# A graph and transformer layer on one core: the message sum moved ahead of the attribute and node products, and the gathers' wait moved from the message to its sum

## The reference

```
h     = (layernorm(x) @ W.T)                       # per node, 8 heads x 32
alpha = h[src].a_src + h[dst].a_dst + sum(relu(attr @ edge_W.T + edge_b) * h[dst])   # per edge and head
alpha = leaky(alpha, 0.2);  ex = exp(alpha - max over the edges of dst)
out   = segment_sum(h[src] * ex / sum of ex over dst, dst)
```

## Time and profile before

| | |
|---|---|
| time before, median of 3 | 4190.25 us (4185.47 to 4199.82) |
| span of the profiled execution | 5158.3 us |
| PE busy | 3767.6 us (73%) |
| DVE busy | 2599.5 us (50%) |
| ACT busy | 2112.2 us (41%) |
| POOL busy | 2005.2 us (39%) |
| mean granted TensorE clock | 0.850 |

### The profile page before, as it was taken

How to read it: one execution, slowest core, us unless ns; L and a number is a source line. 1 busy time by engine, 2 the same in 40 slices (tenths; PEclk the granted TensorE clock), 3 DMA queues, 4 the chain that set the end, 5 groups by cost and what they waited for, 6 DMA issues and landing times.

```text
span 5158.3 us, 88906 instructions
## 1 busy us (share of the span) xinstructions
PE 3767.6 (73%) x22054; PEld 2527.9 (49%) x22055; DVE 2599.5 (50%) x6056; ACT 2112.2 (41%) x5703; POOL 2005.2 (39%) x2172
## 2 busy tenths in 40 slices
PE   4788997677677667677767667777766667891999
PEld 3357886344444444444434444444444444771888
DVE  5556554455555555555555555555555555440111
ACT  3212332344444444444444444444444445442332
POOL 3120000555455544455544555555554442005111
PEclk8889998788888888888888888888888888895999
DMA  4610111333333333333333333443333332102110
GB/s 151 225 44 17 34 33 49 92 99 100 97 97 101 99 99 99 97 100 100 102 100 94 101 100 99 105 102 98 102 102 100 100 101 93 72 22 59 36 36 28
DMA packets 352302, 449.27 MB, mean 87 GB/s; under 512 B 170970, under 2 KB 275163, under 8 KB 350456
## 3 DMA queue, kind: packets, MB, share of 16 engines
q0 software_dynamic: 95568, 267.78, 19.8%
q10 hardware_dynamic: 108050, 122.83, 7.8%
q1 hardware_dynamic: 148231, 53.53, 4.3%
HBM read 389.57 MB, written 55.13 MB: 86 GB/s over the span
## 4 chain that ended last, share of the span: by engine, by line
PE 39%; another core or an unknown queue 17%; issue 15%; DVE 12%; ACT 6%; ACTq 6%; DMA 3%; DVEq 1%; POOL 1%; SPq 0%; POOLq 0%
PE bank L1099 6%; PE bank L1040 5%; PE bank L1183 4%; PE bank L1195 4%; PE bank L1143 3%; PE bank L1005 3%; PE bank L1014 3%; ACT dist L770 3%; DVE prod L1460 3%; PE bank L1061 2%; ACTq L355 2%; DVE msg L1540 2%; ACTq L737 2%; PE bank L1030 2%
## 5 line engine op out<-in xcount | busy, mean ns | idle before, releaser
L514 POOL DMA_INDIRECT al<-h_tab,idx x976 | 975.4, 999 | 1021.5 <-issue 970.8
L752 ACT ACTIVATE enc<-bank,eb 128x512 f32<-128x512 f32 x880 | 555.3, 682 | 1601.5 <-remote 1338.1
L514 POOL DMA_INDIRECT gbuf<-h_tab,idx x784 | 786.5, 1003 | 821.3 <-issue 738.5
L1061 PE MATMUL bank<-prod,hsel 128*32 128x128 f32 x7040 | 336.9, 317 | 928.5 <-issue 779.0
L1040 PE MATMUL bank<-oneh_t,hbt 125*128 125x512 bf16 x2640 | 839.4, 464 | 38.0 <-issue 33.9
L1061 PEld LDWEIGHTS bank<-prod,hsel 128*32 128x32 f32 x7040 | 199.4, 122 | 1098.5 <-issue 916.4
L1460 DVE SCALAR_TENSOR_TENSOR prod<-enc,adst,bank 128x512 f32<-128x512 f32 x880 | 629.1, 736 | 25.8 <-remote 10.9
L1099 PE MATMUL bank<-msg,oneh 128*125 128x264 f32 x2352 | 613.1, 406 | 14.9 <-DVE r L1549 9.1
L1549 DVE TENSOR_TENSOR r<-r,bank 125x264 f32 x440 | 188.5, 428 | 757.8 <-remote 534.3
L1099 PEld LDWEIGHTS bank<-msg,oneh 128*125 128x125 f32 x2352 | 476.8, 204 | 154.4 <-issue 45.9
L770 ACT ACTIVATE dist<-iota_n,dtile 128x125 f32<-128x125 f32 x1760 | 551.1, 384 | 2.0 <-issue 0.5
(11 more groups left out here) (255 smaller groups left out, 5399.6 us busy)
## 6 DMA issues: line engine op xcount, KB each, us to landing
dstb<-dst ACTq DMA_DIRECT2D x440, 125.0 KB
al<-pen_d SPq DMA_DIRECT2D x1760, 4.0 KB
att<-attrx ACTq DMA_DIRECT2D x880, 24.0 KB
al<-h_tab,idx POOLq DMA_INDIRECT x976
link<-links SPq DMA_DIRECT2D x880, 0.2 KB
gbuf<-h_tab,idx POOLq DMA_INDIRECT x784
attrx<-al ACTq DMA_DIRECT2D x8, 1176.0 KB, 12.3
hsplit<-hb POOLq DMA_DIRECT2D x25, 375.0 KB, 5.2
```

Source lines behind the costliest of these rows:

```text
L514: pool.indirect_dma_start(slot(n)[:, c, :], None, h_tab, bass.IndirectOffsetOnAxis(ap=idx[g % 2][:, k:k + 1], axis=0)).then_inc(gathered[n ...
L752: m = act.activation(enc[n % 2][:, k, :], bank[k][:, :], ACT.Relu, bias=eb[:, k:k + 1])
L1061: m = pe.matmul(bank[7][32 * c:32 * c + 32, 0:128], hsel[:, i, :], prod[n % 2][:, k, c * 128:(c + 1) * 128], start=(i == 0 and k == 0), st ...
```

## The change

Two edits. POOL's gather of item n waits for `m_used` instead of `msg_ready`, with the same number: for the message sum of item n-16 on PE rather than for its message on DVE. And in each step of PE `m_sum(k-12)` stands ahead of `e_enc(k)` and `e_dst(k)` instead of behind them.

```
--- before.py
+++ after.py
@@ -507,7 +507,7 @@
                 if n % G == 0:
                     pool.wait_ge(idx_in[g % 2], 64 * (g // 2) + 64)
                 wait(pool, gathered[n % NGS], 64 * (n // NGS))
-                wait(pool, msg_ready, n - RING + 1)
+                wait(pool, m_used, n - RING + 1)
                 pool.sem_inc(went_on, 1)
                 for c in range(4):
                     k = 4 * (n % G) + c
@@ -1117,11 +1117,11 @@
                     g_down((k - 8) // G)
                 if (g := group_at(k, 10)) is not None:
                     g_turn(g)
+                if 0 <= k - LM - 1 < ITEMS:
+                    m_sum(k - LM - 1)
                 if k < ITEMS:
                     e_enc(k)
                     e_dst(k, t[k % EB])
-                if 0 <= k - LM - 1 < ITEMS:
-                    m_sum(k - LM - 1)
```

## The result

The changed kernel takes 4552.87 us (median of 4 runs, 4551.96 to 4558.72) against 4192.72 us for the kernel before beside it (median of 4). The ratio is 1.0846, 95% interval 1.0823 to 1.0869: slower by 360 us. The forecast was 4454 us, with its own range from 4344 to 4586.

A forecast was written before the change was run, and what follows sets the result against it. The edge stage was taken as bound by a PE-ACT ping-pong, 22.5 us a group. PE's reorder at 2.4 us over 110 groups, POOL's gate and the sum's new waits at 0, gave 4190 + 264 = 4454 us, own range 4344 to 4586.

The forecast's parts named there:

- What bounds the kernel: Edge stage: a ping-pong between PE and ACT, neither full, PE waiting for `fac` once a group; 22.5 us a group timed.
- nameless stalls: Edge stage, ahead of ACT's L752: idle time without a releaser, 1338.1 us, read as mostly belonging to the profiled execution.
- The loop before: Edge stage, one group from `fac` to `fac` without stalls: 21.6 us, or 23.1 with step k%4 = 1 at the lower clock.
- PE's A and B: PE's steps with k%4 = 1, 2, 3, 0 are called A, B, C, D; a PE step was taken as 4.8 us.
- The order's cost by step: PE's message sum (1.95 us) ahead of L1030 delays ACT's `enc`: group from 21.6 to 23.9 us, forecast 2.4 a group.
- The clock: PE's step k%4 = 1 begins at 1.2 GHz, message sum 3.57 us: loop from 23.1 to about 26.7, 3.6 us a group.
- POOL's gate at nothing: POOL's gathers waiting for `m_used`: taken as no cost, bounds 0 and +1 us a group.
- the lead: POOL's gathers: place freed in step n-4, rows wanted in n+1, 28 us for 5.3 us of issue plus landing.
- The sum's new waits: PE's message sum waiting for DVE's message and accumulation (L1549): taken at 0, bounded by 0.5 us in each of four steps.
- PE's order indifferent: Rival: PE, the engine most used, is never starved, so only its work counts: 4190 us within 15; chance 0.10.
- DVE freed: Rival: early sum removes waits at DVE's L1549 and PE's L1061: 4029 us, or 4110 if partly on the path; chance 0.10.
- The signs: Changed trace: L1030 some 3 us behind L1061, L752 waits over 137.5 us for L1030, L1549 under 92.8 on L1099.

The follow-up runs named there:

- gate-only trace: Against the kernel before, only POOL's gathers changed, to wait for `m_used`, with PE's order as before: 4213.21 us against 4199.32, ratio 1.0047.
- step A alone: Against the kernel before, message sum ahead only in PE's step k%4 = 1, POOL's gate as before: 4274.70 us, ratio 1.0187.
- C alone: Against the kernel before, message sum ahead only in PE's step k%4 = 3, POOL's gate as before: 4508.86 us against 4202.89, ratio 1.0737.
- the filler run: Against the changed kernel, six node products issued four times in step k%4 = 0: 4371.11 us, ratio 1.0407 to the kernel before.

## Why the prediction was right, and where its steps were not

- *What bounds the kernel.* Right in kind: once a group PE waits for `fac`, and the stage is a chain from PE to ACT and back. The 22.5 us a group that I took for a timed run is 22.8 in the mean of the gate-only trace, 23.0 in the median. The assumption behind it, that being profiled stretches the stage, was wrong in its cause: the gate-only kernel's profiled run took 4203.83 us, no longer than its other runs. Leaving the nameless stalls out of the loop was what made the forecast usable.
- *The loop before.* Its path was right: `fac`, PE's A and B, C's L1030, then ACT's C and D. In the prediction's numbers C's L1030 ends at 11.3 us while ACT has been free since 10.3, and so it is with step A at the lower clock, where the group closes at 23.1 against 23.0 measured. The sizes were near too: PE's A was 4.8 at full clock and measured 6.13 (in two groups of three its products start at 2.4 GHz and go on at 1.2), B 4.51 for 4.8, L1030 of C 1.52 for 1.6, ACT's C 3.86 for 3.7, its reads 1.75, D with `fac` 5.1 for 4.9. ACT idles 1.6 us ahead of B's `enc`.
- *The order's cost by step.* By the loop, A was to take 0.2 us more (the wait for L779), B 0.1 (the wait for L790) and the part of C up to L1030 1.95, together 2.3; the forecast was 2.4, the bounds 1.4 to 3.6. Measured: A 0.98, B 0.23, C 1.98, together 3.2. C and B came out as said; A was mis-sized. Both waits exist: in the changed kernel B starts 0.05 us behind L779 and C 0.05 us behind L790 (medians). The text for step A alone (180 to 210 us, measured 79) goes by the loop with A at the lower clock, which has A's `enc` at 6.0 us; the 65 us for C alone (measured 310) follow from neither loop.
- *The clock.* This is the term that made 2.4 too small. I stayed near the full-clock figure because PE's wait would be nearer 3 us than 10. After the change it is 4.4 us, median, from the last product's end (3.1 in the gate-only kernel; the 6 us in the text of the filler run counted from the message sum's end), L1099 in A takes 3.69 us in the group shown, and the filler takes 180 us back. The clock was a consequence of the change itself: a longer D makes a slower A, also where A's order is untouched (7.13 us with the sum ahead in C alone). The loop with A at the lower clock had 23.1 and 26.7 us; measured are 23.0 and 26.2. The rule of the Trainium skill that I cited, "TensorE: Matmul & The Clock Gate", section "Loop structure matters more than you think", pointed the right way: by it the growth was to be 3.6 us a group, and 3.2 was measured. That the forecast's range held 4553 us is owed to its upper bound, which stood for this case.
- *POOL's gate at nothing.* Nearly: 20 us, inside the bounds of 0 and +1 us a group. The reason I gave, the lead, holds for L759, which does not wait. But POOL was nearer to the loop than the 21.1 us a group that I wrote: its descriptors take 1.09 us on average in the gate-only kernel, not 0.95, which makes 22.2 us of a group of 22.8. That is why the kernel with the attribute product first stops at 21.8. I had not named SP either, whose indices wait for gathers and whose link rows stand behind the indices.
- *The sum's new waits* for the message and the accumulator, taken at 0: 18.3 and 8.5 us on L1549 in the trace after, by the lines of L1099, most of it in step D, and 0.9 us on the message. Right.
- *Rivals.* PE's order indifferent: gone, a reorder of the same work costs 360 us, and by occupancy (PE 80%) one would not see it. DVE freed: L1549's wait for L1099 did fall, from 240.7 us in the gate-only kernel to 148.7 over the whole trace, and the kernel is slower all the same.
- *The signs.* L1030 starts 2.8 to 5.2 us behind L1061 in the group shown, step A's L1061 0.10 us behind `fac`, L752 waits more for L1030, L759 not for DMA: all as said. L1549's wait for L1099, 140.3 us in the edge stage, is not less than the 92.8 of the earlier trace rows; it fell against the gate-only kernel alone. Few of POOL's gathers wait for L1099 by name, 8.5 and 10.7 us in all.
- *Sums.* Four gather sets of 5.3 us are 21.2 us, a third of 161 us leads to 4136 and not 4110 (which is a half), and 7.8 us a group lead to 5048 and not 5000. None of it moves the forecast.

## What to carry to other kernels

When an instruction moves within an engine's step, ask which of the others' starts it now stands in front of; the cost is its length times the places where that start is on the path, and here one step in four bore nine tenths of it. Put ahead what starts another engine and needs nothing new: one small product moved to the front of each step gained 110 us. And an idle stretch of TensorE is paid twice when the work behind it runs at 1.2 GHz; where a change lengthens the wait, price the work after it at the lower clock too.

## What was not expected of the hardware

- Filler products made the changed kernel faster by some 180 us: 18 more products of 512 columns a group, and the message sum behind them fell from 3.69 to 2.02 us.
- POOL's gather descriptors take 1000 ns on average at 31 us a group, 1046 to 1048 at 26.1 (the kernel after), 1085 to 1092 at 22.8 (gate only) and 1051 to 1071 at 21.8 (attribute product first). Pace alone does not order them. With the gate on `msg_ready` they are shorter at the same pace: 1014 to 1028 with the order alone changed (26.0 us a group), 1057 to 1078 with the sum between the two products (22.9). Why is not shown.
